# Four tiles in flight, transposes by DMA, and the threshold search moved to GpSimd

## Chip, cores, metric

One core of one Trainium2 chip. The metric is the device time of one launch in microseconds; of several runs the median is given.

## What is computed

2048 rows of 512 floats go through three blocks, each with a layer norm in front and a residual behind:

```python
x = x + 0.5 * lora_ffn(layernorm(x))   # FFN1: 64 experts of rank 16, top 16 by router score
x = x + glu(layernorm(x))              # gate, sparsify, up, down, width 1376
x = x + 0.5 * lora_ffn(layernorm(x))   # FFN3: the same weights as FFN1
# lora_ffn: scores = x @ Wr.T; gates = softmax(top 16 scores); h = x A.T;
#           out = (h * gates) B * 2
# glu: s = silu(x @ w_gate.T); in each row, the 688 smallest |s| of 1376 are set to 0;
#      out = (s * (x @ w_up.T)) @ w_down.T
```

## The kernel before

The rows are cut into 16 tiles of 128. All weights stay in SBUF, each as an f16 pair (hi, lo), and every product is three matmuls (`three`, lines 351 to 353: hi·hi, lo·hi, hi·lo). At the start each weight matrix is loaded in pieces, squared on ACT and summed on PE to find its scale, and split into hi (ACT, line 530) and lo (DVE, line 685). Then a loop of steps runs, i = 2 to 17. Step i does FFN1 and gate/up of tile i, finds the threshold of tile i-1, and does down and FFN3 of tile i-2. Every engine has its own in-order program; semaphores are the only order between engines.

PE, in a step: experts of FFN1 (`experts`, 24 matmuls of 512 columns and 12 of 64), `down` (33 matmuls), `combine` of FFN1 (24), experts of FFN3, the gate product and the up product (`wide`, 36 each), `combine` of FFN3. The three normed inputs are transposed on PE (`turn_x`, line 378, four f32 transposes each); the routed expert outputs and the masked values are transposed by DMA from SP's queue (`turn_p`, `turn_v`).

The threshold of a tile is found by seven counts on ACT (`count`, line 554: a Sign over 1376 columns with a sum) with six small correction steps between them (`search`, lines 755 to 759, four linked operations on 128x1 on DVE). `select` (lines 813 to 816) takes the exact threshold from the candidates, `mark` (lines 822 to 831) makes the mask, and branches to `bisect` if any row missed its count; for that it reduces flags and loads four values into registers. `mask` (863) multiplies, ACT casts to hi (584), DVE makes lo (876). The gate path is tanh on ACT (566), `silu` on DVE (847), `magnitude` on ACT (571), `gated` on DVE (855). GpSimd (POOL) does only the inverse square roots of the norms (`rstd`, lines 326 and 329).

`mag` has two buffers, so the magnitudes of tile i are made while the search on tile i-1 is in use. In DVE's program the six `search` steps stand between other work of the step:

```python
choose(1, i); median(0); route(1, i); median(1); apply_route(1, i); median(2)
p_split(1, i - 2); ...; norm_stats(3, x2); median(3); norm_apply(3, ...); median(4)
xt_to_lo(3, ...); ...; median(5); ...; select(i, b)
```

## Time and profile before

| | |
|---|---|
| median of 3 runs | 898.3 us (897.61 to 902.42) |
| the profiled execution | 900.5 us, its span 898.5 us |
| PE busy | 753.2 us, 84% |
| DVE busy | 571.4 us, 64% |
| ACT busy | 360.9 us, 40% |
| POOL busy | 36.3 us, 4% |
| mean granted TensorE clock | 0.943 of full speed |

The page's slices show three parts: a start of some 157 us, in which PE is busy for about half of the time; fourteen steps of about 46 us with PE at 90% and more; and two last steps, for tiles 14 and 15, in which PE is again half busy. A matmul's busy time overlaps with its neighbour's, so starts are compared, not durations.

### The profile page before, as it was taken

The page shows a single profiled execution, that of the slowest core. Times are in us where ns is not written, and L with a number is a line of the kernel's source. Part 1 is how long each engine was busy: PE and PEld are TensorE (multiplying, and loading weights), DVE is VectorE, ACT ScalarE, POOL GpSimd, SP SyncE. Part 2 cuts the span into 40 slices and gives each one's busy share as a digit, 9 for nine tenths or more (in the row PEclk, how much of TensorE's full clock was granted, in tenths as well). Part 3 has the DMA queues.
Part 4 walks back from the last instruction along what each step waited for, and adds up shares of the span by engine and source line. Part 5 has one row for each costly group of instructions (what it writes and reads, how often), then busy time and mean ns, then how long its engine had stood idle before and what let it go on. Part 6 is the DMA issues. An engine that isn't in the chain of part 4 may idle for free.

```text
span 898.5 us, 10482 instructions
## 1 busy us (share of the span) xinstructions
PE 753.2 (84%) x3863; PEld 356.3 (40%) x3863; DVE 571.4 (64%) x1403; ACT 360.9 (40%) x449; POOL 36.3 (4%) x104
## 2 busy tenths in 40 slices
PE   2766570999999898999999999999989999985555
PEld 0322230454545454444444444444444545442122
DVE  5355547576767676768686767676775767663521
ACT  4235574434343434343434343434434353433100
POOL 0000000000000000000000000000000000000000
PEclk9977795899999999999999999999999999997777
DMA  6332100213131313131312121212221221212121
GB/s 216 127 137 81 57 1 6 51 24 79 24 80 24 80 24 80 24 80 24 79 25 68 34 61 33 68 36 68 36 68 24 54 49 40 53 34 34 24 44 35
DMA packets 118922, 49.17 MB, mean 55 GB/s; under 512 B 110832, under 2 KB 110832, under 8 KB 118864
## 3 DMA queue, kind: packets, MB, share of 16 engines
q1 hardware_dynamic: 118864, 48.45, 22.8%
q8 instruction: 30, 0.49, 0.2%
q14 instruction: 28, 0.23, 0.1%
HBM read 16.97 MB, written 4.19 MB: 24 GB/s over the span
## 4 chain that ended last, share of the span: by engine, by line
PE 74%; DVE 10%; DMA 6%; issue 4%; ACT 4%; SPq 2%; DVEq 0%; POOL 0%; POOLq 0%; ACTq 0%
PE ps L351 24%; PE ps L352 23%; PE ps L353 23%; DMA vt_hi<-stage 3%; PE ps L378 2%; DVE xt_lo L702 1%; ACT xt_hi L535 1%; DMA pt_lo<-stage 1%; DMA stage<-w_a 1%; DMA vt_lo<-stage 1%; DVE y L931 1%; DVE w_d_lo L685 1%; PE ps L364 1%; ACT signs L554 1%; DVE small L655 1%
## 5 line engine op out<-in xcount | busy, mean ns | idle before, releaser
L554 ACT ACTIVATE signs<-mag,small 128x1376 bf16<-128x1376 f32 x112 | 161.4, 1441 | 144.8 <-DVE small L759 141.6
L351 PE MATMUL ps<-w_b_hi,pt_hi 128*128 128x512 f16 x256 | 100.0, 391 | 24.1 <-DMA pt_lo<-stage 16.5
L351 PE MATMUL ps<-w_d_hi,vt_hi 128*128 128x512 f16 x176 | 68.8, 391 | 38.3 <-issue 24.2
L351 PE MATMUL ps<-w_a_hi,xt_hi 128*128 128x512 f16 x256 | 100.3, 392 | 0.0
L352 PE MATMUL ps<-w_a_hi,xt_lo 128*128 128x512 f16 x256 | 100.0, 391 | 0.0
L352 PE MATMUL ps<-w_b_hi,pt_lo 128*128 128x512 f16 x256 | 99.9, 390 | 0.0
L353 PE MATMUL ps<-w_b_lo,pt_hi 128*128 128x512 f16 x256 | 99.7, 389 | 0.0
L353 PE MATMUL ps<-w_a_lo,xt_hi 128*128 128x512 f16 x256 | 99.6, 389 | 0.0
L351 PE MATMUL ps<-w_g_hi,xt_hi 128*128 128x512 f16 (+1 forms) x192 | 69.3, 361 | 8.7 <-DVE w_g_lo L685 6.1
L351 PE MATMUL ps<-w_u_hi,xt_hi 128*128 128x512 f16 (+1 forms) x192 | 69.4, 361 | 6.5 <-DVE w_u_lo L685 6.1
L352 PE MATMUL ps<-w_g_hi,xt_lo 128*128 128x512 f16 (+1 forms) x192 | 69.5, 362 | 0.0
L352 PE MATMUL ps<-w_u_hi,xt_lo 128*128 128x512 f16 (+1 forms) x192 | 69.5, 362 | 0.0
L353 PE MATMUL ps<-w_g_lo,xt_hi 128*128 128x512 f16 (+1 forms) x192 | 69.4, 361 | 0.0
L353 PE MATMUL ps<-w_u_lo,xt_hi 128*128 128x512 f16 (+1 forms) x192 | 69.3, 361 | 0.0
L352 PE MATMUL ps<-w_d_hi,vt_lo 128*128 128x512 f16 x176 | 69.0, 392 | 0.0
L353 PE MATMUL ps<-w_d_lo,vt_hi 128*128 128x512 f16 x176 | 68.7, 391 | 0.0
L890 DVE SCALAR_TENSOR_TENSOR x<-ps,small,x 128x512 f32<-128x512 f32 x16 | 12.0, 751 | 76.6 <-PE ps L353 76.6
L571 ACT ACTIVATE mag<-gate 128x1376 f32<-128x1376 f32 x16 | 21.6, 1350 | 86.2 <-DVE gate L847 86.2
L745 DVE TENSOR_TENSOR routed<-ps,weight 128x1024 f32<-128x1024 f32 x32 | 39.1, 1221 | 21.3 <-PE ps L353 21.3
L535 ACT ACTIVATE xt_hi<-ps 128x512 f16<-128x512 f32 x48 | 28.3, 590 | 56.4 <-PE ps L378 56.4
L566 ACT ACTIVATE gate<-ps,small 128x1376 f32<-128x1376 f32 x16 | 22.5, 1404 | 65.2 <-PE ps L353 65.2
L351 PEld LDWEIGHTS ps<-w_b_hi,pt_hi 128*128 128x128 f16 x256 | 25.6, 100 | 55.4 <-issue 31.2
(115 smaller groups left out, 1186.9 us busy)
## 6 DMA issues: line engine op xcount, KB each, us to landing
xin<-x SPq DMA_DIRECT2D x16, 256.0 KB, 3.0
out<-y SPq DMA_DIRECT2D x16, 256.0 KB, 2.0
stage<-w_g SPq DMA_DIRECT2D x4, 688.0 KB, 5.9
stage<-w_u SPq DMA_DIRECT2D x4, 688.0 KB, 5.9
stage<-w_d SPq DMA_DIRECT2D x5, 512.0 KB, 6.2
stage<-w_a SPq DMA_DIRECT2D x4, 512.0 KB, 7.2
stage<-w_b SPq DMA_DIRECT2D x4, 512.0 KB, 9.2
pt_hi<-stage SPq DMA_TRANSPOSE x30, 3.2
```

What stands on the lines that cost most here:

```text
L351: pe.matmul(dst, x_hi, w_hi, start=start, stop=False)
L352: pe.matmul(dst, x_lo, w_hi, start=False, stop=False)
L353: return pe.matmul(dst, x_hi, w_lo, start=False, stop=stop)
L364: mm = pe.matmul(bank(m.bank + o // BANK, w), ones[0:rows, :], sq[0:rows, q * m.width + o:q * m.width + o + w], start=c + q == 0, stop=c + ...
L378: mm = pe.transpose(bank(0, P, c * P), normed[j][:, c * P:(c + 1) * P], ident[:, :])
L535: act.activation(xt_hi[j][:, :, :], bank(0).rearrange("p (c t) -> p c t", c=DC), ACT.Copy).then_inc(xt_hi_ready[j], 1)
L554: act.activation(signs[:, :], mag[1 - b][:, :], ACT.Sign, bias=thr, scale=-1.0, accum_out=bal).then_inc(counted, 1)
L566: act.activation(gate[:, :], bank(2, I), ACT.Tanh, scale=unscale_g).then_inc(tanh_ready, 1)
L571: act.activation(mag[b][:, :], gate[:, :], ACT.Abs, accum_out=mag_sum).then_inc(mag_ready, 1)
L655: read = dve.tensor_reduce(norm2, bank(m.bank, m.width), AX.X, ALU.max)
L745: dve.tensor_tensor(routed[:, :].rearrange("p (k r) -> p k r", r=RANK), ps[:, 5 * BANK:5 * BANK + KR].rearrange("p (k r) -> p k r", r=RANK ...
L890: dve.scalar_tensor_tensor(out=x2[:, :], in0=bank(1), scalar=unscale_m, in1=x1[b][:, :], op0=ALU.mult, op1=ALU.add).then_inc(out_read, 1)
```

## The change

The loop is written anew. Step d (from -1 to 15) does down and FFN3 of tile d, the threshold, mask, up and `gated` of tile d+1, the gate product, `silu` and `magnitude` of tile d+2, the norm before the gate of tile d+3, FFN1 of tile d+5 and its norm for tile d+6 (`LEAD` = 4). FFN1 of tiles 0 to 4 stands in the start. From d = 11 on there is no FFN1 left, and `emit` takes its second branch on each engine.

- The inputs are split to f16 hi and lo in SBUF (`x_to_hi` ACT, `x_to_lo` DVE) and both halves are turned by one DMA transpose (`turn_x` on SP's queue), three more per tile. PE's transposes are gone.
- `search` and the first guess (`aim`) are on GpSimd, as six linked operations in place of four. All six searches of a tile stand one after another there, with `rstd(3, d)` after the third.
- There is one `mag`, one `val` and one `gate` buffer. Gate and up products share PSUM banks 2 to 4; the down product has bank 0, combine bank 1.
- `select` now works out whether the row failed; a matmul with ones adds the flags over the rows (`sum_flags`), and `check` loads one value and branches once. `mask` compares and multiplies in one operation.
- Weights b, g, u and d are loaded from GpSimd's queue, and GpSimd makes some of the lo pieces of g, u and d.
- x is loaded into nine slots, several tiles ahead, and results are added in place.

```diff
+LEAD = 4
+
+SLOTS = 9
...
+    calls = [(1, t) for t in range(LEAD + 1)]
+    for d in range(NT):
+        calls += [(1, d + LEAD + 1)] if d + LEAD + 1 < NT else []
+        calls += [(3, d)]
+    number = {c: k for k, c in enumerate(calls)}
...
+        DOWN, COMB, WIDE, EXP, SCORE = 0, 1, 2, 5, 7
...
+            def turn_x(j, t):
...
+                sp.dma_start_transpose(dst[:, :, :], halves[j]).then_inc(xt_loaded[j], 16)
...
+            def aim(t):
+
+                pool.wait_ge(mag_ready, t + 1)
+                link(pool.tensor_scalar(step, mag_sum, -SPACING / 2, None, ALU.mult))
+                pool.tensor_scalar(thr, mag_sum, GUESS, None, ALU.mult).then_inc(thr_ready, 1)
+
+            def search(t, n):
+
+                pool.wait_ge(counted, ROUNDS * t + n + 1)
+                link(pool.tensor_scalar(off, bal, -7.0, None, ALU.add))
+                link(pool.tensor_scalar(far, off, off, 7.5 ** 2, ALU.mult, ALU.is_gt))
+                link(pool.tensor_tensor(move, off, far, ALU.mult))
+                link(pool.tensor_tensor(move, move, step, ALU.mult))
+                link(pool.tensor_scalar(move, move, DAMP[n], None, ALU.mult))
+                pool.wait_ge(thr_ready, ROUNDS * t + n + 1)
+                pool.tensor_tensor(thr, thr, move, ALU.add).then_inc(thr_ready, 1)
+
+            def emit(d):
+                f = first(d)
+                for n in range(ROUNDS - 1):
+                    if n == 3 and d >= 0:
+                        rstd(3, d)
+                    if d + 1 < NT:
+                        search(d + 1, n)
+                if f is not None and f + 1 < NT:
+                    rstd(1, f + 1)
+                if d + 3 < NT:
+                    rstd(2, d + 3)
+                if d + 2 < NT:
+                    aim(d + 2)
+
...
+            def sum_flags(t):
+
+                if t:
+                    pe.wait_ge(x2_ready, t)
+                pe.wait_ge(flag_ready, t + 1)
+                pe.matmul(bank(DOWN, 1), ones[:, :], flag[:, 0:1], start=True, stop=True
+                          ).then_inc(flag_summed, 1)
+
+            def emit(d):
+                f = first(d)
+                if d >= 0:
+                    down(d)
+                if f is not None:
+                    experts(1, f)
+                if d == -1:
+                    norms(MD)
+                if d + 1 < NT:
+                    ups(d + 1, d == -1)
+                if f is not None:
+                    if d >= 0:
+                        experts(3, d)
+                    sum_flags(d + 1)
+                    combine(1, f)
+                    if d + 2 < NT:
+                        gates(d + 2)
                 else:
-                    turn_x(3, i - 2)
...
-            def search(i, n):
-
-
-                dve.wait_ge(counted, ROUNDS * (i - 1) + n + 1)
-                link(dve.tensor_scalar(off, bal, -7.0, None, ALU.add))
-                link(dve.tensor_scalar(far, off, off, 7.5 ** 2, ALU.mult, ALU.is_gt))
-                link(dve.scalar_tensor_tensor(out=move, in0=off, scalar=far, in1=step,
-                                              op0=ALU.mult, op1=ALU.mult))
-                dve.scalar_tensor_tensor(out=thr, in0=move, scalar=DAMP[n], in1=thr,
-                                         op0=ALU.mult, op1=ALU.add).then_inc(thr_ready, 1)
...
+            def select(t):
+
+
...
+                dve.wait_ge(counted, ROUNDS * (t + 1))
+                if t:
+                    dve.wait_ge(v_hi_ready, t)
+                    dve.wait_ge(v_lo_ready, t)
+                link(dve.scalar_tensor_tensor(out=masked[:, 0:I], in0=mag, scalar=thr, in1=mag,
+                                              op0=ALU.is_le, op1=ALU.mult))
+                link(dve.max(cand8, masked[:, 0:I]))
+                link(dve.scalar_tensor_tensor(out=top_a, in0=evens, scalar=bal, in1=cand8,
+                                              op0=ALU.is_equal, op1=ALU.mult, accum_out=kth))
+                link(dve.tensor_scalar(greater, cand8, kth, None, ALU.is_gt, ALU.add,
+                                       accum_out=above))
+                link(dve.scalar_tensor_tensor(out=wrong, in0=above, scalar=2.0, in1=bal,
+                                              op0=ALU.mult, op1=ALU.not_equal))
+                link(dve.scalar_tensor_tensor(out=wrong, in0=bal, scalar=15.0, in1=wrong,
+                                              op0=ALU.is_gt, op1=ALU.max))
+                if t:
+                    dve.wait_ge(flag_summed, t)
+                dve.scalar_tensor_tensor(out=flag[:, 0:1], in0=cand8[:, 0:1], scalar=thr,
+                                         in1=wrong, op0=ALU.is_equal, op1=ALU.max
+                                         ).then_inc(flag_ready, 1)
+
+            def mask(t):
+                dve.wait_ge(val_ready, t + 1)
+                link(dve.scalar_tensor_tensor(out=masked[:, 0:I], in0=mag, scalar=kth, in1=val,
+                                              op0=ALU.is_gt, op1=ALU.mult))
+
...
+            def check(t):
+                dve.wait_ge(flag_summed, t + 1)
+                link(dve.tensor_copy(flagged, bank(DOWN, 1)))
+                bad = dve.value_load(flagged[0:1, :], min_val=0, max_val=P)
+                with dve.If(bad != 0):
+                    bisect()
+                dve.memset(spare[:, 4:5], 0.0).then_inc(masked_ready, 1)
...
+            def emit(d):
+                f = first(d)
+                if f is not None:
+                    k1 = number[1, f]
+                    if d >= 0:
+                        k3 = number[3, d]
+                        if d >= 1:
+                            add_ffn(3, d - 1)
+                        add_down(d)
+                        norm_stats(3, d)
+                    choose(k1)
+                    if d >= 0:
+                        norm_apply(3, d)
+                    route(k1)
+                    if d >= 0:
+                        x_to_lo(3, d)
+                    apply_route(k1)
+                    p_to_lo(k1)
+                    select(d + 1)
+                    if d >= 0:
+                        choose(k3)
+                    gated(d + 1)
+                    if d >= 0:
+                        route(k3)
+                        apply_route(k3)
+                    mask(d + 1)
+                    if d >= 0:
+                        p_to_lo(k3)
+                    check(d + 1)
+                    v_to_lo(d + 1)
+                    add_ffn(1, f)
+                    if f + 1 < NT:
+                        norm_stats(1, f + 1)
+                    norm_stats(2, d + 3)
+                    if f + 1 < NT:
+                        norm_apply(1, f + 1)
+                        x_to_lo(1, f + 1)
+                    norm_apply(2, d + 3)
+                    x_to_lo(2, d + 3)
+                    silu(d + 2)
+                    return
+                k3 = number[3, d]
...
+                median(0, 1, 2, 3)
+                if f is not None:
+                    exps(number[1, f])
+                if d >= 0:
+                    x_to_hi(3, d)
+                if f is not None:
+                    median(4, 5)
+                    p_to_hi(number[1, f])
+                    median(6)
+                    if d >= 0:
+                        exps(number[3, d])
+                        p_to_hi(number[3, d])
+                    v_to_hi(d + 1)
+                    if f + 1 < NT:
+                        x_to_hi(1, f + 1)
+                    x_to_hi(2, d + 3)
+                    tanh(d + 2)
+                    magnitude(d + 2)
```

Where the instructions stand. First the search, on DVE before, within one step of the loop (L755 to L759 is one search step, L813 and L815 are `select`):

```order
L697 TENSOR_SCALAR normed<-x_0,mv,rvar 128x512
L736 SCALAR_TENSOR_TENSOR chosen,small<-work,expd 128x64
L739 RECIPROCAL small<-small 128x1
L740 TENSOR_SCALAR weight<-chosen,small 128x64
L755 TENSOR_SCALAR small<-small 128x1
L756 TENSOR_SCALAR small<-small 128x1
L757 SCALAR_TENSOR_TENSOR small<-small 128x1
L759 SCALAR_TENSOR_TENSOR small<-small 128x1
L702 TENSOR_TENSOR xt_lo<-ps,xt_hi 128x512
L745 TENSOR_TENSOR routed<-ps,weight 128x1024
L813 SCALAR_TENSOR_TENSOR stage<-mag,small 128x1376
L815 MAX small<-stage 128x8
```

And on GpSimd after the change (L395 to L401 is one search step, L379 and L383 are `rstd`):

```order
L399 TENSOR_SCALAR small<-small 128x1
L401 TENSOR_TENSOR small<-small 128x1
L379 TENSOR_SCALAR rvar<-mv 128x1
L383 TENSOR_TENSOR rvar<-rvar,neg_half 128x1
L395 TENSOR_SCALAR small<-small 128x1
L396 TENSOR_SCALAR small<-small 128x1
L397 TENSOR_TENSOR small<-small 128x1
L398 TENSOR_TENSOR small<-small 128x1
L399 TENSOR_SCALAR small<-small 128x1
L401 TENSOR_TENSOR small<-small 128x1
```

The search step went from four operations in DVE's program to six in GpSimd's, with nothing but `rstd` between one and the next. Second, DVE at the end of a step, before (L847 `silu`, L863 `mask`, L855 `gated`, L931 the residual of FFN3), from just behind the branch:

```order
L697 TENSOR_SCALAR normed<-xin,mv,rvar 128x512
L847 SCALAR_TENSOR_TENSOR gate<-gate,ps 128x1376
L863 TENSOR_TENSOR stage<-stage,keep 128x1376
L855 SCALAR_TENSOR_TENSOR stage<-gate,ps 128x1376
L859 TENSOR_SCALAR small<-small 128x1
L860 TENSOR_SCALAR small<-small 128x1
L702 TENSOR_TENSOR xt_lo<-ps,xt_hi 128x512
L931 SCALAR_TENSOR_TENSOR y<-ps,small,x 128x512
L876 TENSOR_TENSOR stage<-stage 128x1408
```

and after, also from just behind the branch (L968 `v_to_lo`, L857 residual of FFN1, L800 to L812 the norms and splits of the tiles to come, L870 `silu`):

```order
L962 MEMSET spare 128x1
L968 TENSOR_TENSOR mem<-mem 128x1408
L857 SCALAR_TENSOR_TENSOR x<-ps,small,x 128x512
L800 BN_STATS stats<-x 128x6
L801 BN_AGGR mv<-stats 128x2
L800 BN_STATS stats<-mem 128x6
L801 BN_AGGR mv<-stats 128x2
L805 TENSOR_SCALAR normed<-x,mv,rvar 128x512
L812 TENSOR_TENSOR halves<-normed,halves 128x512
L805 TENSOR_SCALAR normed<-mem,mv,rvar 128x512
L812 TENSOR_TENSOR halves<-normed,halves 128x512
L870 SCALAR_TENSOR_TENSOR mem<-mem,ps 128x1376
```

`silu` of the next tile, which the next search waits for, stood second behind the branch and is now the twelfth and last of the step.

## Rows read from the trace of the kernel before

**Rows 1.** Windows view: us of window, busy us of each engine, PE clock, DMA share, GB/s.

```profile
0.00:157.50 157.50, 83.08 (x369) 35.17 (x370) 83.85 (x184) 75.30 (x81) 4.56 (x18) 0.83 0.25 89
342.90:620.01 277.11, 264.87 (x1428) 129.24 (x1425) 197.18 (x492) 116.35 (x150) 13.28 (x36) 1.00 0.24 51
```

**Rows 2.** Timeline, ACT, one search round: start us, us, line, operation.

```profile
811.89 1.44 ACT L554 ACTIVATE signs<-mag,small 128x1376 bf16<-128x1376 f32 x1 [0.92 <-DVE small L759]
...
814.34 1.44 ACT L554 ACTIVATE signs<-mag,small 128x1376 bf16<-128x1376 f32 x1 [0.92 <-DVE small L759]
```

**Rows 3.** Timeline, DVE, the same round.

```profile
813.46 0.15 DVE L755 TENSOR_SCALAR small<-small 128x1 f32<-128x1 f32 x1 [1.60 <-ACT signs L554]
...
814.15 0.16 DVE L759 SCALAR_TENSOR_TENSOR small<-small 128x1 f32<-128x1 f32 x1
```

**Rows 4.** Timeline, POOL (GpSimd), one pair of small operations.

```profile
452.13 0.19 POOL L326 TENSOR_SCALAR rvar<-mv 128x1 f32<-128x1 f32 x1 [28.26 <-DVE mv L693]
452.40 0.55 POOL L329 TENSOR_TENSOR rvar<-rvar,neg_half 128x1 f32<-128x1 f32 x1
```

**Rows 5.** Groups by line, DVE: busy us, mean ns of one, idle before.

```profile
L745 DVE TENSOR_TENSOR routed<-ps,weight 128x1024 f32<-128x1024 f32 x32 | 39.1, 1221 | 21.3 <-PE ps L353 21.3
L702 DVE TENSOR_TENSOR xt_lo<-ps,xt_hi 128x512 f16<-128x512 f32 x48 | 32.9, 685 | 2.7 <-ACT xt_hi L535 2.1
L813 DVE SCALAR_TENSOR_TENSOR stage<-mag,small 128x1376 f32<-128x1376 f32 x16 | 26.3, 1642 | 2.2 <-ACT signs L554 2.2
L863 DVE TENSOR_TENSOR stage<-stage,keep 128x1376 f32<-128x1376 f32 x16 | 25.4, 1585 | 6.8 <-issue 6.8
L692 DVE BATCH_NORM_STATS2 stats<-x 128x6 f32<-128x512 f32 x32 | 22.2, 694 | 1.1
L697 DVE TENSOR_SCALAR normed<-x,mv,rvar 128x512 f32<-128x512 f32 x32 | 17.5, 546 | 5.3 <-POOL rvar L329 4.8
L890 DVE SCALAR_TENSOR_TENSOR x<-ps,small,x 128x512 f32<-128x512 f32 x16 | 12.0, 751 | 76.6 <-PE ps L353 76.6
```

**Rows 6.** Groups by line, ACT.

```profile
L549 ACT ACTIVATE stage<-routed 128x1024 f16<-128x1024 f32 x30 | 31.5, 1050 | 23.2 <-DVE routed L745 23.2
L566 ACT ACTIVATE gate<-ps,small 128x1376 f32<-128x1376 f32 x16 | 22.5, 1404 | 65.2 <-PE ps L353 65.2
L571 ACT ACTIVATE mag<-gate 128x1376 f32<-128x1376 f32 x16 | 21.6, 1350 | 86.2 <-DVE gate L847 86.2
```

**Rows 7.** Timeline, DVE, around the branch of line 831.

```profile
424.97 0.18 DVE L828 TENSOR_REDUCE ints<-flags_t 128x1 int32<-128x32 f32 x1
428.81 0.55 DVE L697 TENSOR_SCALAR normed<-xin,mv,rvar 128x512 f32<-128x512 f32 x1 [3.66 <-issue]
```

**Rows 8.** Timeline, DVE, choose and route of tile 14, last tile but one.

```profile
829.45 0.23 DVE L723 COPY scores<-ps 128x64 f32<-128x64 f32 x1 [0.98 <-PE ps L353]
...
831.75 0.15 DVE L755 TENSOR_SCALAR small<-small 128x1 f32<-128x1 f32 x1
```

**Rows 9.** Timeline, PE, matmuls after a pause.

```profile
858.67 0.58 PE L351 MATMUL ps<-w_d_hi,vt_hi 128*128 128x512 f16 x1 [6.75 <-DMA vt_lo<-stage]
859.05 0.63 PE L352 MATMUL ps<-w_d_hi,vt_lo 128*128 128x512 f16 x1
859.47 0.63 PE L353 MATMUL ps<-w_d_lo,vt_hi 128*128 128x512 f16 x1
```

**Rows 10.** Timeline, PE, matmuls later in the same stretch.

```profile
866.80 0.38 PE L351 MATMUL ps<-w_d_hi,vt_hi 128*128 128x512 f16 x1
867.02 0.38 PE L352 MATMUL ps<-w_d_hi,vt_lo 128*128 128x512 f16 x1
```

**Rows 11.** Chain that ended last: select of tile 0 and of tile 15.

```profile
143.00 1.66 DVE stage L813
...
836.87 1.57 DVE stage L813
```

**Rows 12.** DMA view: transposes, KB and median us to landing.

```profile
pt_lo<-stage SPq DMA_TRANSPOSE x30, 3.1
vt_lo<-stage SPq DMA_TRANSPOSE x16, 3.9
```

1209 lines of the change are left out of this document (590 added, 619 removed).

## The prediction, made before the change was run

> **What bounds the kernel now.** I read the windows first. In the six steps from 342.90 to 620.01 us a step takes 277.11 / 6 = 46.2 us, with 264.87 / 6 = 44.1 us of PE busy at full clock [rows 1]: PE bounds the steps. In the first 157.5 us it is busy for only 83 us [rows 1], since there it waits for weights to be scaled and split. The chain of waits gives the frame for the sum. `select` of tile 0 starts at 143.0 and that of tile 15 at 836.9 [rows 11]: 15 intervals of 46.3 us, and behind the last one 898.5 - 836.9 = 61.6 us. So the span is start + 15 intervals + tail = 143.0 + 693.9 + 61.6.
>
> The timelines show what a search costs alone. One Sign count starts 2.45 us behind the other [rows 2]; DVE's four operations take 0.85 of that, from 813.46 to 814.31 [rows 3]. In the steps this is hidden: there are two `mag` buffers, and DVE's other work stands between the six search steps.
>
> **PE's work after the change.** The transposes of x leave. Matmuls of 512 columns follow each other at 0.215 us at full clock [rows 10]. A step has 177 of them, 24 of 352 columns (0.15, by columns) and 24 of 64 (0.03): 38.1 + 3.6 + 0.7 = 42.4 us. If PE still bounded the steps, 3.8 us of 46.2 would go. The question is whether anything else takes over.
>
> **The new cycle.** With one `mag` buffer, `magnitude` of tile t+1 must follow `mask` of tile t, and the search on t+1 must follow that; DVE's program puts twelve pieces of work between `select` and `silu`. I follow one interval of a full step from the start of `select` on, in us, all in series on DVE unless named:
> - `select`: two passes over 1376 (1.64 and about the same [rows 5]) and five small operations (0.2 to 0.3 each, as in [rows 3]): 4.6.
> - choose and route of FFN3: 831.75 - 829.45 = 2.3 [rows 8]. `gated` 1.5, `apply_route` 1.15, `mask` 1.6 [rows 5]; `p_to_lo` of 1024 elements 1.15, as `apply_route`. Together 7.7.
> - `check`: a copy and a memset 0.4, and one load with its branch. Now four loads and the branch leave DVE idle for 3.66 us [rows 7]. One costs between a quarter of it (0.9) and all of it; I take 1.5, nearer the quarter since three of four loads are gone. 1.9.
> - `v_to_hi` on ACT 1.45 (like the tanh of nearly the same size, [rows 6]), then `v_to_lo` 1.55: 3.0.
> - `add_ffn` 0.75, two stats with their aggregates 1.75, and 0.1 of waiting for POOL [rows 4, 5]: 2.6.
> - Norm and hi/lo of two inputs in turn, ACT between: 0.5 + 0.65 + 0.65 + 0.5 + 0.65 [rows 5]; hi of 512 elements is priced from 1.05 for 1024 [rows 6]: 3.0.
> - tanh 1.45 [rows 6], `silu` 1.65, `magnitude` 1.6 with its accumulator read [rows 6], `aim` on POOL 0.6 (two operations 0.27 apart [rows 4], and a crossing): 5.3.
>
> That is 28.1. Then the search, which nothing shortens: seven counts and six steps. A count with its read is 813.43 - 811.89 = 1.54 [rows 2, 3]. On POOL a linked tensor_scalar costs 0.27 from start to start [rows 4]. No row shows a plain tensor_tensor there. It is bounded by the tensor_scalar's 0.19 and by the 0.55 of the power function [rows 4]; I take 0.25, nearer the lower end, because the power is another function, while DVE's small operations hardly differ with their operands [rows 3]. A step: 3 x 0.27 + 2 x 0.33 + 0.25 = 1.72 (1.54 to 2.62). With 0.15 for the two crossings a round is 1.54 + 1.72 + 0.15 = 3.41 (3.23 to 4.31), against 2.45 now. The search: 6 x 3.41 + 1.6 = 22.1. **A full interval is 50.2 us**, 4 longer than now.
>
> The page "GPSIMD Engine Reference" of the Trainium skill (section 3.1, Elementwise) measures a two-input tensor_tensor at 1.96 times DVE's time; an estimate by it puts one at 0.16 x 1.96 = 0.31, the interval at 51.3 and the time at 921. No row here shows it.
>
> PE is covered by this. From `sum_flags` (4.8 behind `select`) it does combine 5.2 and the gate product 7.0, so tanh could start at 17.2, but ACT comes to it only at 22.7. `down`, both experts and the up product also fit; PE would idle for some 7.8 us a step. The DMA transposes need 3.1 to 3.9 us each [rows 12], are issued four and more us ahead of their use except for the input of FFN3, whose experts PE reaches about 4 us too early, and that wait ends before the flags are ready. SP's queue holds nine issues in 50 us. The other work DVE does ahead of `select` (norms, routing of FFN1) lies beside the counts.
>
> **Last steps and ends.** From d = 11 on FFN1 is gone and `silu` stands right behind `v_to_lo`: 4.6 + 1.6 + 2.2 + 3.0 + 1.6 + 1.6 + 0.6 + 22.1 = 37.3. The intervals are: the first without FFN3's part, 50.2 - 4.6; ten full ones; the last with FFN1 without the norm of a next tile, 50.2 - 2.9; three of 37.3. Sum 45.6 + 502.0 + 47.3 + 111.9 = 706.8, where 693.9 stood.
>
> Start: three more tiles of FFN1 (16 us at full clock before the first `magnitude`) go into PE's idle time, and loads run ahead; against this, ACT squares and splits w_d before it counts, POOL makes three lo pieces (no row for such an operation there), and the seven counts no longer overlap. I keep 143, with 10 to either side, and 20 shorter as a rival.
>
> Tail: `select` to the down product is 15.5 (4.6 + 1.6 + 2.2 + 3.0 and 4.1 for the DMA) where 858.67 - 836.87 = 21.8 stood [rows 9, 11]; turning the input of FFN3 by DMA costs 2.4 more. 61.6 - 6.3 + 2.4 = 57.7.
>
> Span 143 + 706.8 + 57.7 = 907.5. The profiled execution takes 2.0 more than its span (900.5 against 898.5) and lies 2.2 above the median, so the median comes to 907.5 + 2.0 - 2.2 = 907.3: **908 us**. Each us of the full interval is worth 12. The point of balance is 49.4.
>
> **Rivals.**
> 1. GpSimd's small operations are cheaper when linked one to another than the pair shown: at 0.2 each from start to start a step is 1.2, a round 2.9, the interval 47.1, the time **871**. It decides from a round of 3.28 down, close to the low end of my bound. For it: DVE's own chain has gaps of 0.04 only. Against: 0.27 is measured on the same kind of link [rows 4].
> 2. GpSimd and DVE collide. `x_to_lo` of FFN3 (0.69) and `p_to_lo` (1.22) [rows 5] fall into a search step, and each may hold it for its length: up to 1.9 an interval, **931**. Nothing in the trace speaks for or against; POOL is busy for 36 us in all and never beside such an operation. The Trainium skill, page "SBUF — State Buffer", section "SBUF: two separate sides", says that a DVE operation with two SBUF inputs and a GpSimd operation lock each other out for a whole instruction, which is this case.
> 3. PE falls to half clock in its new gaps. After a pause of 6.75 us matmuls follow at 0.42 to 0.43 instead of 0.215 [rows 9, 10]. Two pauses of 3 to 4 us a step are short, and 5.5 us of slack hide a few slow matmuls; if combine and gate product ran wholly at half clock (24.4 instead of 12.2), the interval would grow by 6.7: **988**, or 948 if in every second step.
> 4. The start shrinks by 20: the products for five tiles fill it and the counts begin right behind `magnitude`: **888**. PE's 74 idle us [rows 1] speak for it, ACT's order against.
> 5. Tensor_tensor on GpSimd has the price of the power function, 0.55: round 4.31, interval 55.6, **973**.
> 6. The order of DVE does not bind, and PE bounds: 42.4 to 43 a full interval, about **820**. The serial walk speaks against it.
>
> **How the numbers follow.** This kernel's measurement can tell about 0.5% (4.5 us) from no change. Chances: forecast 0.40 (its own range 896 to 920; 0.12 of it within 0.5%, the rest slower), rival 1 0.20, rival 2 0.17, rival 3 0.07, rival 4 0.08, rival 5 0.04, rival 6 0.04. Faster 0.32, same 0.12, slower 0.56. The range, 868 to 962, leaves out rival 6, what of rival 1 goes beyond its price, and rivals 5 and 3 at their worst, some 0.2 in all.
>
> **What would show it.** Right: `select` to `select` 50 us in the middle; POOL busy for over 130 us; ACT's counts 3.4 us apart without a break, waiting for POOL; PE at 84% in the steps, with waits at the flag matmul and at the experts of FFN3; 37 us intervals at the end. Wrong: counts under 3.2 or over 3.7 apart; tanh waiting for PE instead of ACT's own order; PE over 95% busy; a first `select` before 130 or after 155.

## The result, and the profile after

| | before | after |
|---|---|---|
| median | 897.95 us (896.99 to 902.42) | 948.19 us (945.28 to 949.11) |
| ratio | | 1.054, 95% interval 1.050 to 1.059 |
| span of the profiled execution | 898.5 us | 947.3 us |
| PE / DVE / ACT / POOL busy | 84 / 64 / 40 / 4% | 79 / 51 / 38 / 25% |
| mean granted TensorE clock | 0.943 | 0.908 |

The change makes the kernel 5.4% slower; I had forecast 908 us, 1.1% slower. The windows answer [rows 1]: us of the window, busy us of PE, PEld, DVE, ACT and POOL, the TensorE clock, DMA share, GB/s. The first window is the start up to the first `select`, the second ten full steps.

```profile
0.00:162.67 162.67, 86.95 (x403) 35.96 (x403) 86.92 (x183) 75.09 (x81) 68.66 (x90) 0.84 0.44 117
210.32:717.85 507.53, 449.67 (x2260) 208.56 (x2260) 274.32 (x580) 194.12 (x250) 120.21 (x440) 0.94 0.31 61
```

POOL is busy for 68.66 us in the start, where it had been busy for 4.56. A full step is now 50.75 us. The chain that ended last gives the frame, as in [rows 11]: start us, duration, `select` (L889) of tiles 0, 1, 2, 7, 8, 11 to 15.

```profile
162.67 1.66 DVE mem L889
210.32 1.66 DVE mem L889
260.77 1.66 DVE mem L889
...
514.55 1.67 DVE mem L889
565.25 1.66 DVE mem L889
...
717.85 1.67 DVE mem L889
765.43 1.66 DVE mem L889
808.85 1.66 DVE mem L889
852.30 1.66 DVE mem L889
891.52 1.67 DVE mem L889
```

Set against the sum of the prediction:

| part | forecast | measured | difference |
|---|---|---|---|
| start, to the first `select` | 143.0 | 162.7 | +19.7 |
| first interval | 45.6 | 47.6 | +2.0 |
| ten full intervals | 502.0 | 507.5 | +5.5 |
| last interval with FFN1 | 47.3 | 47.6 | +0.3 |
| three late intervals | 111.9 | 126.1 | +14.2 |
| tail | 57.7 | 55.8 | -1.9 |
| span | 907.5 | 947.3 | +39.8 |

So the long middle is as forecast, and 34 of the missing 40 us lie in the start and in the late intervals. The first interval is 2.0 over its forecast too; what it lost was not traced. The timelines show the rest.

**The search round** (ACT, then POOL; answers to [rows 2] and [rows 4]; start us, us):

```profile
545.41 1.44 ACT L645 ACTIVATE signs<-mem,small 128x1376 bf16<-128x1376 f32 x1 [1.84 <-POOL small L401]
...
548.78 1.44 ACT L645 ACTIVATE signs<-mem,small 128x1376 bf16<-128x1376 f32 x1 [1.84 <-POOL small L401]
```

```profile
543.65 0.21 POOL L395 TENSOR_SCALAR small<-small 128x1 f32<-128x1 f32 x1 [1.65 <-ACT signs L645]
543.96 0.30 POOL L396 TENSOR_SCALAR small<-small 128x1 f32<-128x1 f32 x1
544.34 0.19 POOL L397 TENSOR_TENSOR small<-small 128x1 f32<-128x1 f32 x1
544.61 0.19 POOL L398 TENSOR_TENSOR small<-small 128x1 f32<-128x1 f32 x1
544.88 0.22 POOL L399 TENSOR_SCALAR small<-small 128x1 f32<-128x1 f32 x1
545.18 0.19 POOL L401 TENSOR_TENSOR small<-small 128x1 f32<-128x1 f32 x1
```

A round is 3.37 us (forecast 3.41), the six operations 545.18 + 0.19 - 543.65 = 1.72 (forecast 1.72). That the second number comes out to the hundredth is luck. I had the three tensor_scalars too cheap: from start to start they take 0.31, 0.38 and 0.30, not 0.27 each, since `L396`, with a column as scalar, takes 0.30 by itself. And I had the three tensor_tensors too dear: they take 0.19 like a plain tensor_scalar, not 0.25. The two errors are 0.18 each and cancel.

**The collision.** At the end of the same search POOL (first fence) and DVE (second):

```profile
561.88 1.21 POOL L398 TENSOR_TENSOR small<-small 128x1 f32<-128x1 f32 x1
```

```profile
561.81 1.22 DVE L850 TENSOR_TENSOR p_lo<-routed,p_hi 128x1024 f16<-128x1024 f32 x1 [5.14 <-ACT p_hi L640]
```

An operation of 0.19 us stands for 1.21, until `p_to_lo` ends. Rival 2 was built on the Trainium skill, page "SBUF — State Buffer", section "SBUF: two separate sides": a DVE operation with two inputs in SBUF, or one in a 2-port mode, and a GpSimd operation that reads SBUF shut each other out for the whole instruction. The trace agrees for the first kind. One search pays 1.0 for this and 0.3 for `x_to_lo` of FFN3. From first count to `select` it takes 23.2 us (542.03 to 565.25) where 22.1 were forecast.

**The branch** (DVE, answers to [rows 7]): one load and branch leave 1.54 us idle, for which I had 1.5.

```profile
526.68 0.15 DVE L958 CAST ints<-ps 128x1 int32<-128x1 f32 x1
528.37 0.06 DVE L962 MEMSET spare<- 128x1 f32 x1 [1.54 <-issue]
```

**The start.** POOL makes seven lo pieces, two operations each. Here are the two operations of the first piece of w_g, the rstd that stands behind both pieces of w_g, and the first operation of a piece of w_u; then DVE:

```profile
67.23 3.81 POOL L372 TENSOR_SCALAR mem<-mem,small 128x1376 f32<-128x1376 f32 x1 [15.52 <-ACT w_g_hi L622]
71.12 2.79 POOL L373 TENSOR_TENSOR w_g_lo<-mem,w_g_hi 128x1376 f16<-128x1376 f32 x1
...
80.61 0.19 POOL L379 TENSOR_SCALAR rvar<-mv 128x1 f32<-128x1 f32 x1
...
98.55 3.76 POOL L372 TENSOR_SCALAR mem<-mem,small 128x1376 f32<-128x1376 f32 x1
```

```profile
81.56 0.55 DVE L805 TENSOR_SCALAR normed<-x,mv,rvar 128x512 f32<-128x512 f32 x1 [16.86 <-POOL rvar L383]
...
98.58 4.01 DVE L805 TENSOR_SCALAR normed<-x,mv,rvar 128x512 f32<-128x512 f32 x1 [0.97 <-POOL rvar L383]
...
103.17 7.98 DVE L783 SCALAR_TENSOR_TENSOR w_u_lo<-mem,small,w_u_hi 128x1376 f16<-128x1376 f32 x2
```

Such a piece costs POOL 6.6 us (3.81 + 2.79), against 1.6 on DVE (3.21 for the two that it makes at 83.15). DVE waits 16.86 us for an rstd that was queued behind two pieces. Later DVE's own operations stretch beside POOL's: 4.01 instead of 0.55, 7.98 instead of 3.2. The first search then waits for the pieces of w_d: count 0 is at 130.74, its step at 141.26, count 1 at 143.16.

**The late intervals** (ACT, step of tile 12's `select` at 765.43):

```profile
777.52 1.35 ACT L657 ACTIVATE mem<-mem 128x1376 f32<-128x1376 f32 x1 [1.90 <-DVE mem L870]
...
781.42 1.06 ACT L640 ACTIVATE p_hi<-routed 128x1024 f16<-128x1024 f32 x1 [2.12 <-DVE routed L840]
786.10 0.63 ACT L629 ACTIVATE halves<-normed 128x512 f16<-128x512 f32 x1 [3.63 <-DVE normed L805]
786.64 1.43 ACT L645 ACTIVATE signs<-mem,small 128x1376 bf16<-128x1376 f32 x1
```

`magnitude` ends at 779, but ACT's program has exps and `p_to_hi` of FFN3 and `x_to_hi(2)` ahead of the next count, and each waits for DVE. The first count comes 21.2 us after `select`; the walk of the prediction had 15.2.

### The profile page after: what moved, and what is told of

It reads as the page before. It is cut to its first block, busy times and chain, and to the rows that moved or that the text cites. A ratio compares the mean times of both kernels' runs of the same rounds, so it can differ in the third digit from the quotient of the medians.

```text
span 947.3 us, 10462 instructions
## 1 busy us (share of the span) xinstructions
PE 752.4 (79%) x3671; PEld 341.7 (36%) x3671; DVE 487.4 (51%) x1008; ACT 361.3 (38%) x447; POOL 241.4 (25%) x742
## 4 chain that ended last, share of the span: by engine, by line
DVE 30%; ACT 24%; POOL 20%; issue 14%; PE 7%; DMA 3%; DVEq 1%; POOLq 0%; SPq 0%; ACTq 0%
ACT signs L645 14%; POOL small L398 3%; POOL small L396 3%; DVE mem L889 3%; DVE small L891 3%; DVE mem L870 3%; DVE mem L968 3%; POOL small L399 2%; DVE routed L840 2%; PE ps L454 2%; POOL small L395 2%; ACT mem L663 2%; POOL small L397 2%; PE ps L455 2%; ACT mem L657 2%
## 5 line engine op out<-in xcount | busy, mean ns | idle before, releaser
L645 ACT ACTIVATE signs<-mem,small 128x1376 bf16<-128x1376 f32 x112 | 161.4, 1441 | 189.3 <-POOL small L401 181.6
L454 PE MATMUL ps<-w_a_hi,xt_f 128*128 128x512 f16 x256 | 102.4, 400 | 8.4 <-DVE routed L840 6.0
L455 PE MATMUL ps<-w_a_hi,xt_f 128*128 128x512 f16 x256 | 101.8, 398 | 0.0
L456 PE MATMUL ps<-w_a_lo,xt_f 128*128 128x512 f16 x256 | 100.9, 394 | 0.0
L379 POOL TENSOR_SCALAR rvar<-mv 128x1 f32<-128x1 f32 x48 | 9.1, 190 | 338.7 <-DVE mv L801 336.3
L454 PE MATMUL ps<-w_d_hi,mem 128*128 128x512 f16 x176 | 68.8, 391 | 9.9 <-DMA mem<-mem 9.9
L850 DVE TENSOR_TENSOR p_lo<-routed,p_hi 128x1024 f16<-128x1024 f32 x32 | 39.2, 1224 | 69.1 <-ACT p_hi L640 68.7
L454 PE MATMUL ps<-w_g_hi,xt 128*128 128x512 f16 (+1 forms) x192 | 68.5, 357 | 0.9 <-DVE mem L876 0.8
L455 PE MATMUL ps<-w_d_hi,mem 128*128 128x512 f16 x176 | 68.9, 391 | 0.0
L454 PE MATMUL ps<-w_u_hi,xt 128*128 128x512 f16 (+1 forms) x192 | 68.5, 357 | 0.0
L456 PE MATMUL ps<-w_g_lo,xt 128*128 128x512 f16 (+1 forms) x192 | 68.5, 357 | 0.0
L456 PE MATMUL ps<-w_u_lo,xt 128*128 128x512 f16 (+1 forms) x192 | 68.5, 357 | 0.0
L455 PE MATMUL ps<-w_u_hi,xt 128*128 128x512 f16 (+1 forms) x192 | 68.5, 357 | 0.0
L455 PE MATMUL ps<-w_g_hi,xt 128*128 128x512 f16 (+1 forms) x192 | 68.5, 357 | 0.0
L456 PE MATMUL ps<-w_d_lo,mem 128*128 128x512 f16 x176 | 68.4, 388 | 0.0
L395 POOL TENSOR_SCALAR small<-small 128x1 f32<-128x1 f32 x96 | 20.7, 215 | 147.0 <-ACT signs L645 146.9
```

What stands on the lines that cost most here:

```text
L395: link(pool.tensor_scalar(off, bal, -7.0, None, ALU.add))
L454: pe.matmul(dst, x_hi, w_hi, start=start, stop=False)
L455: pe.matmul(dst, x_lo, w_hi, start=False, stop=False)
L456: return pe.matmul(dst, x_hi, w_lo, start=False, stop=stop)
L645: act.activation(signs[:, :], mag, ACT.Sign, bias=thr, scale=-1.0, accum_out=bal).then_inc(counted, 1)
L850: dve.tensor_tensor(p_lo[:, :], routed[:, :], p_hi[:, :], ALU.subtract).then_inc(p_lo_ready, 1)
```

## Experiments

Each ratio is to the kernel before, with its 95% interval; all but e6 start from the changed kernel. "Full interval" is from `select` to `select` in the middle steps, "late" the three last (43.42, 43.45 and 39.22 in the changed kernel).

**e1: all lo pieces on DVE.**

```diff
-    MG = Matrix("g", DC, I, 1, P, AT_G, 2, (1, 3))
+    MG = Matrix("g", DC, I, 1, P, AT_G, 2, ())
-    MU = Matrix("u", DC, I, 1, P, 0, 2, (1, 3))
+    MU = Matrix("u", DC, I, 1, P, 0, 2, ())
-    MD = Matrix("d", IC, D, 2, LAST, AT_G, 0, (1, 3, 5))
+    MD = Matrix("d", IC, D, 2, LAST, AT_G, 0, ())
...
-            split_lo(MG, 1)
-            split_lo(MG, 3)
...
-            split_lo(MU, 1)
-            split_lo(MU, 3)
```

> The changed kernel, with all lo pieces of the weights made on DVE again (seven pieces less on GpSimd). Theory (GpSimd's pieces lengthen the start: 13.2 us of pieces of w_g stand ahead of rstd, and DVE waits 16.9 us for it; pieces of w_d stand ahead of the first search step, and ACT waits 10.9 us): the first select starts at 143 to 148 instead of 162.7, the intervals behind it stay, and the time is 928 to 934. Rival (the start is bound by the loads and by PE's work for five tiles, the waits only show where the slack is): first select at 158 or later, 943 to 948.

Measured: 922.9 us, ratio 1.029 (1.022 to 1.036). The first `select` starts at 134.58 instead of 162.67, and nothing else moves (full intervals 50.7, late 43.4, 43.4, 39.2). The gain is larger than expected, but not all of the 28.1 us of the start is due to the pieces. The third rstd, which stands ahead of the first piece, starts at 31.39 in the changed kernel's profiled execution and at 27.90 in this one. From it to the first `select` there are 131.3 and 106.7 us. So the pieces cost 24.6 us, which fits the medians (948.2 - 922.9 = 25.3). That is all of the excess of the start over my 143, and 5 more.

**e2: the search step in four GpSimd operations.**

```diff
-                link(pool.tensor_tensor(move, off, far, ALU.mult))
-                link(pool.tensor_tensor(move, move, step, ALU.mult))
-                link(pool.tensor_scalar(move, move, DAMP[n], None, ALU.mult))
+                link(pool.tensor_scalar(move, far, off, step, ALU.mult, ALU.mult))
                 pool.wait_ge(thr_ready, ROUNDS * t + n + 1)
-                pool.tensor_tensor(thr, thr, move, ALU.add).then_inc(thr_ready, 1)
+                pool.tensor_scalar(thr, move, DAMP[n], thr, ALU.mult, ALU.add).then_inc(thr_ready, 1)
```

> The changed kernel, with a search step of four GpSimd operations instead of six, for the same result: the product of three factors and the damped sum are one tensor_scalar each with two scalars. Theory (the six rounds are in series with everything else in every interval): the rounds go from 3.38 to about 2.9 us, each interval loses 6 x 0.5 = 3 us, 16 searches give 48 us, and the time is 900 (895 to 908). Rival A (PE bounds the steps and the waits for the flags only show slack): within 5 us of 948. Rival B (GpSimd's two-scalar operations cost more than they save): 940 to 955.

Measured: 914.5 us, ratio 1.019 (1.016 to 1.022), of the expected gain 34 us instead of 48. POOL's timeline shows one step:

```profile
528.69 0.22 POOL L395 TENSOR_SCALAR small<-small 128x1 f32<-128x1 f32 x1 [1.66 <-ACT signs L643]
529.01 0.29 POOL L396 TENSOR_SCALAR small<-small 128x1 f32<-128x1 f32 x1
529.40 0.34 POOL L397 TENSOR_SCALAR small<-small 128x1 f32<-128x1 f32 x1
529.84 0.26 POOL L399 TENSOR_SCALAR small<-small 128x1 f32<-128x1 f32 x1
```

A step is 1.41 us: the operation with two columns as scalars costs 0.34 and the one with a column and a constant 0.26, more than the plain ones that they replace. A round is 3.07 and the full interval 48.8, so each 0.31 us of a round is worth 1.9 to 2.0 an interval: the search is in series with everything, as the prediction has it.

**e4: `p_to_lo` with one input in memory** (the low half of p is replaced by a scaled copy of `routed`, so that this part is not computed).

```diff
-                dve.tensor_tensor(p_lo[:, :], routed[:, :], p_hi[:, :], ALU.subtract
+                dve.tensor_scalar(p_lo[:, :], routed[:, :], unscale_r, 0.0, ALU.mult, ALU.mult
```

> The changed kernel, with p_lo made from routed alone by a tensor_scalar (one SBUF input instead of two; the low halves of the routed values are not what the reference needs, so the precision of both FFN blocks changes). Theory (a DVE operation with two SBUF inputs shuts GpSimd out): the one long GpSimd operation in every search (L398, 1.21 us where its neighbours take 0.19) falls back to about 0.2, intervals with FFN1 lose 1.0 us, 12 us in all: 936. Rival (the long operation has another cause, such as its place behind five rounds): L398 keeps one of 1.2 us in every search and the time stays at 948.

Measured: 935.5 us, ratio 1.042 (1.038 to 1.046); the full interval is 49.94. The time fits by luck: the trace shows another reason than the expected one. `p_to_lo` takes 0.75 us instead of 1.22, and POOL's operation beside it still stands for all of it:

```profile
504.93 0.73 POOL L398 TENSOR_TENSOR small<-small 128x1 f32<-128x1 f32 x1
```

So the form with one input holds POOL too, for as long as it runs. Whether this is the 2-port mode that the Trainium skill names, no run here tells. The 0.8 us that an interval wins are about what `p_to_lo` is shorter by, 0.47 in DVE's chain and 0.48 in POOL's.

**e5: the late order of ACT.**

```diff
-                median(0, 1, 2, 3)
+                if d >= 1 and first(d - 1) is None:
+                    median(0)
+                    exps(number[3, d - 1])
+                    median(1)
+                    p_to_hi(number[3, d - 1])
+                    median(2, 3)
+                    if d + 2 < NT:
+                        x_to_hi(2, d + 2)
+                else:
+                    median(0, 1, 2, 3)
```

On POOL rstd(2) of these steps stands behind search 2, ahead of search 3.

> Edit: in the late steps only (those without an FFN1 of a later tile), exps and the high half of the routing of the tile's FFN3, and x_to_hi(2), are taken out of ACT's program ahead of the next search and stand behind its counts 0, 1 and 3; rstd(2) goes with search 3 on GpSimd. Theory: the three late intervals are 43.42, 43.45 and 39.22 us because count 0 of the next search stands behind exps, p_to_hi and x_to_hi(2), which wait for TensorE, though aim was done 6 to 7 us sooner (aim about 780, first count 786.64); freed of that they take 37 to 38 us each, as forecast: 933 us (930 to 937). Rival: TensorE's FFN3 of the tile waits for the high half of p that comes later now and the end moves by as much: 945 to 950.

Measured: 944.1 us, ratio 1.050 (1.046 to 1.054); the late intervals are 41.43, 41.43 and 37.52, together 5.7 us less. (The span of the profiled execution is only 1.9 less, 945.4. Its first `select` is at 167.70, and its third rstd is already 4.8 later than in the changed kernel, with the same instructions up to there.) The first half of the theory holds: the first count comes 14.2 us behind `select` instead of 21.2. But 5 of these 7 us are lost again inside the search. TensorE's waits did not grow (flag 5.09 and 4.55 us in the first two late steps, where it was 5.08 and 5.08, and 1.1 and 1.3 for the transposed values where it was 2.7 and 2.3), so it is not the rival either. DVE's timeline, then POOL's:

```profile
797.05 0.55 DVE L815 TENSOR_SCALAR normed<-x,mv,rvar 128x512 f32<-128x512 f32 x1 [4.14 <-POOL rvar L383]
```

```profile
796.17 0.19 POOL L379 TENSOR_SCALAR rvar<-mv 128x1 f32<-128x1 f32 x1
...
800.68 0.19 POOL L379 TENSOR_SCALAR rvar<-mv 128x1 f32<-128x1 f32 x1 [3.66 <-DVE mv L811]
```

I had put rstd(2) a search step too late on POOL. DVE stood for it, reached the addition and the norm of FFN3 late, and rstd(3) of that norm stands ahead of the next search step: count 4 followed count 3 by 7.75 us. e9 has this mended.

**e7: the search back on DVE**, in the four operations of the kernel before, at six places of DVE's program.

```diff
+                    search(d + 1, 0, 1)
                     if d >= 0:
                         add_down(d)
                         norm_stats(3, d)
                     choose(k1)
+                    search(d + 1, 2)
                     if d >= 0:
                         norm_apply(3, d)
+                    search(d + 1, 3)
                     route(k1)
                     if d >= 0:
                         x_to_lo(3, d)
                     apply_route(k1)
+                    search(d + 1, 4)
                     p_to_lo(k1)
+                    search(d + 1, 5)
```

> Edit: the change with only its search step put back on DVE in the four instructions of the kernel before, at hand-chosen places of DVE's program (two steps ahead of add_down, one behind choose, one behind norm_apply, one behind apply_route, one behind p_to_lo); the overlap of four tiles, the lead and the DMA turns stay. Theory: a round takes 3.38 us on GpSimd and took 2.45 on DVE, so six rounds give 5.6 us of the 50.7 back wherever the search sets the interval, less what DVE's other work holds a step up; TensorE at about 45 to 48 then bounds the full intervals: 48 x 11, three late ones 5 less each, first one 5 less, start 2 less: 948 - 30 - 15 - 7 = 896 us (885 to 908), so the move of the search alone is all of the loss and the overlap of four tiles is worth nothing beside the kernel before. Rival: the long interval comes from the order of the tail (routing, check, norms, silu in a row), which stays: the steps on DVE are held up by its other work and no more than 20 us come back, 928 to 948.

Measured: 894.5 us, ratio 0.994 (0.991 to 0.997). The number is as expected: with the search on DVE the whole loss is gone, and the kernel is 0.6% below the one before. But the move of the search is not the only loss. In the profiled executions this kernel's start is still 17.1 us longer than before (160.05 against 143.00), its 15 intervals are 10.4 shorter and its tail is 6.1 shorter, and e1 won 25 us with the search left on GpSimd. So the change had two large losses, search and start, and gains in the loop and the tail that cover about one of them. What the DMA transposes, the longer lead and the single buffers are worth one by one was not tried. The full interval is 47.9 and the late ones are 38.64, 38.03 and 39.35. Not each round is short, since DVE's other work holds steps up (ACT's counts):

```profile
521.93 1.44 ACT L632 ACTIVATE signs<-mem,small 128x1376 bf16<-128x1376 f32 x1 [0.92 <-DVE small L961]
...
524.38 1.44 ACT L632 ACTIVATE signs<-mem,small 128x1376 bf16<-128x1376 f32 x1 [0.92 <-DVE small L961]
...
528.26 1.44 ACT L632 ACTIVATE signs<-mem,small 128x1376 bf16<-128x1376 f32 x1 [2.35 <-DVE small L961]
```

**e6: the kernel before with only its search on GpSimd**, in the six operations of the change, with the two `mag` buffers and the old order kept (POOL's program; DVE's calls of `search` go).

```diff
+                median(0, 1, 2)
                 rstd(3, i - 2, turn)
+                median(3, 4)
                 if cur:
                     rstd(2, i, turn + 1)
+                median(5)
```

> The kernel before, with its six search steps moved to GpSimd as in the change, and nothing else. Theory (a search step on GpSimd costs 0.9 us more, but in the kernel before the search lies beside other work, with two buffers for mag): within 5 us of 898, the rounds that stand alone at the end give the few us, PE stays at 44 of 46 us. Rival (GpSimd's steps cost by themselves, wherever they stand: 6 x 0.9 us an interval): 960 to 980.

Measured: 934.9 us, ratio 1.043 (1.038 to 1.047). Both numbers miss. I had thought that two buffers hide a longer search, since the search of one tile is not in series with the making of the next. Steps are 47.8 us for 46.1, with some of 50 to 53. The waits of TensorE (us in total, times, longest), first before, then e6:

```profile
PE ps L351 <- DVE xt_lo L702: 33.2, 19, 16.6
```

```profile
PE ps L379 <- DVE xt_lo L730: 64.2, 19, 19.1
```

TensorE waits 31 us longer for lo halves of inputs, about the 33 us by which the span grew. ACT makes hi halves between its counts: at 459.06 it counts, the next count waits for POOL until 467.16, whose step stood behind an rstd at 464.15, and the hi half of FFN3's input follows at 468.60. A late search step thus reaches TensorE through ACT's queue. How much of this is the price of the steps, and how much the two places of rstd between them, was not tried.

**e3 and e11: the next gate early.** In full steps `silu` of the next tile moves on DVE right behind `v_to_lo`, tanh and `magnitude` on ACT go ahead of `x_to_hi(1)` and `x_to_hi(2)`, `aim` on POOL ahead of the rstds. e3 on ACT, and then e11 against e3 on DVE:

```diff
+                if d >= 0 and first(d - 1) is not None:
+                    median(0)
+                    if first(d - 1) + 1 < NT:
+                        x_to_hi(1, first(d - 1) + 1)
+                    median(1)
+                    x_to_hi(2, d + 2)
+                    median(2, 3)
...
-                    if f + 1 < NT:
-                        x_to_hi(1, f + 1)
-                    x_to_hi(2, d + 3)
                     tanh(d + 2)
                     magnitude(d + 2)
```

```diff
                     v_to_lo(d + 1)
-                    silu(d + 2)
                     add_ffn(1, f)
+                    silu(d + 2)
```

> Edit: in the full steps only, the next tile's gate is made ready sooner. On DVE silu(d+2) stands right behind v_to_lo(d+1) instead of behind add_ffn, the two normed and the two halves of x; on ACT tanh and magnitude stand ahead of x_to_hi(1) and x_to_hi(2), which move behind count 0 and count 1 of the next search; on GpSimd aim stands ahead of the two rstd. The work and its cost stay the same. Theory: the full interval of 50.7 us is a chain through DVE (select, choose, route, V, add_ffn, norms, silu) into ACT and GpSimd, so 5 us of work taken out of the chain shorten each of the 11 full intervals by about 5: 893 us (885 to 905). Rival 1: TensorE's work and the granted clock (busy 449.67 of 507.5 us over ten intervals, clock 0.94) bound the interval at about 45 to 46 already, and the moved high halves come late for TensorE, which then waits for them instead: at most 1 us each, 937 to 948. Rival 2: the search shares its engine ACT with the moved halves, and the rounds grow by what they take: no gain, 945 to 955.

> Edit: e3 (tanh, magnitude and silu of the next tile early, search in six operations, low halves still shared with GpSimd) with add_ffn of FFN1 ahead of silu on DVE instead of behind it, and nothing else. Theory: what e3 lacked to its forecast was TensorE's wait of 3.9 us in each full step for the bank that this add frees, with the fall of the granted clock that goes with waits; without it the full interval is the search's again, 44.66 of the combined kernel plus six rounds times 0.31: 46.5 us instead of 49.5, 11 of them: 934 - 33 = 901 us (893 to 912). Rival: the combined kernel needed the shorter rounds for its gain, and with 3.38 us in a round the order of the add matters by its own 0.7 us at most: 925 to 940.

Measured: e3 934.2 us, ratio 1.040 (1.037 to 1.043); e11 926.4 us, ratio 1.032 (1.029 to 1.034). Full intervals are 49.6 (in turn 48.9 and 50.0) and 48.5 where 45.7 and 46.5 were expected. In e3 two things go wrong in a row, on PE and then on POOL:

```profile
530.67 0.58 PE L456 MATMUL ps<-w_b_hi,pt_hi 128*128 128x512 f16 x1 [3.87 <-DVE x L864]
```

```profile
546.52 0.19 POOL L379 TENSOR_SCALAR rvar<-mv 128x1 f32<-128x1 f32 x1 [3.29 <-DVE mv L808]
```

TensorE waits for the bank that `add_ffn` frees, `down` comes late, and the search stands behind rstd(3), which waits for it. e11 takes this away, and its interval still doesn't reach 46.5. What is left is a loop through TensorE, read under e9.

**e8: everything together**: e1, e2, e3 and e5 in one kernel.

> Edit: the early silu, the late order, the search step of four operations and the low halves of the weights on DVE, all in one kernel. Theory: the gains add as long as DVE, ACT and GpSimd's chain is the bound: start 132 to 135, first interval 43, eleven full intervals near 44 where the chain alone asks for 50.7 - 1.9 - 5 = 43.8 and TensorE was busy for 45.0 in each at clock 0.94, so 45 to 46 each, late ones 35.5 each, tail 55: 134 + 43 + 11 x 45.5 + 106.5 + 55 = 839 us (825 to 860), faster than the kernel before (898). Rival: the gains do not add, since TensorE waits for the same flags in another place or its clock falls when it stands in longer stretches of waiting: 870 to 900, no better than the kernel before.

Measured: 877.8 us, ratio 0.978 (0.974 to 0.981). Faster than before, but 39 over the expectation: full intervals of 48.2 instead of 45.5 (the wait of e3, 3.9 us a step) and late ones of 39.6, 39.6 and 35.5 (the misplaced rstd(2) of e5).

**e9: e8 with both mended.** On DVE the pair of e11; on POOL and ACT, in the late steps, against e8:

```diff
-                    if n == 3 and d >= 1 and first(d - 1) is None and d + 2 < NT:
+                    if n == 2 and d >= 1 and first(d - 1) is None and d + 2 < NT:
                         rstd(2, d + 2)
...
-                    median(2, 3)
+                    median(2)
                     if d + 2 < NT:
                         x_to_hi(2, d + 2)
+                    median(3)
```

> Edit, on the combined kernel (877.8 us): on DVE add_ffn of FFN1 stands ahead of silu(d+2) instead of behind it; in the late steps rstd(2) stands ahead of search 2 on GpSimd instead of behind it, and x_to_hi(2) behind count 2 instead of count 3. Theory: TensorE waits 3.9 us in each full step for the bank that this add_ffn frees, while DVE waits for tanh ahead of it; with the add first the wait falls to about 1.5, and as TensorE bounds the full step there (44.35 of 48.22 us busy) 2.3 us are won in each of 11; in the late steps DVE stood 4.1 us behind rstd(2), of which 3 to 3.5 come back in three of them: 877.8 - 25 - 10 = 843 us (837 to 855). Rival: the chain through gate, tanh, silu and the search is the bound and not TensorE, so that moving the add (0.74 us) ahead of silu only delays the chain: full intervals 48.2 to 49, 868 to 886.

Measured: **841.0 us, ratio 0.935 (0.929 to 0.941)**, as expected, the fastest kernel of the study. All full intervals are 44.65 to 44.70, the late ones 37.23, 37.23 and 35.45. TensorE is close to being the bound (the window 230 to 650, columns as above):

```profile
230.00:650.00 420.00, 400.90 (x2101) 189.46 (x2102) 259.02 (x545) 180.46 (x232) 104.50 (x291) 1.00 0.36 68
```

That is 95% busy at full clock, and [rows 1] had the same 95% at 46.2 us a step: here the transposes are gone from TensorE. But it is not the bound by itself. It is busy for 42.9 of the 44.66 us of a step and still waits 1.05 for the flags, and tanh waits 1.8 for it: the interval is a loop through search, flags, gate product and tanh.

Beside e11 this shows the loop. For each of three kernels, the changed one, e11 and e9, follow TensorE's wait at the flag matmul (timeline) and then the window of the 12.4 us behind it (combine and gate product):

```profile
519.16 0.16 PE L556 MATMUL ps<-flag,ones 128*128 128x1 bf16 x1 [5.47 <-DVE flag L902]
```

```profile
519.15:531.55 12.40, 12.39 (x49) 5.22 (x50) 9.11 (x19) 2.87 (x3) 0.00 (x0) 0.82 0.26 52
```

```profile
505.94 0.16 PE L558 MATMUL ps<-flag,ones 128*128 128x1 bf16 x1 [3.85 <-DVE flag L909]
```

```profile
505.93:518.33 12.40, 12.39 (x51) 5.36 (x52) 9.11 (x19) 2.87 (x3) 0.00 (x0) 0.86 0.26 51
```

```profile
498.12 0.16 PE L554 MATMUL ps<-flag,ones 128*128 128x1 bf16 x1 [1.05 <-DVE flag L913]
```

```profile
498.12:510.52 12.40, 12.40 (x61) 5.87 (x61) 9.11 (x19) 2.87 (x3) 0.00 (x0) 1.00 0.27 52
```

Behind a wait of 3.85 or 5.47 us the granted clock of the stretch is 0.86 or 0.82, a mixture of the levels 2.4 and 1.2 GHz; behind 1.05 it is 1.00, and 61 matmuls fit in where 49 to 51 did. In the changed kernel tanh starts 22.4 behind `select` with no idle time of ACT before it, so it waits for ACT's own order. In e11 and e9 ACT stands idle before tanh, for 3.2 to 5.0 us in e11 and mostly 1.8 in e9, until the gate product ends: now that product is in the loop. In e11 tanh starts 18.8 us behind `select` (501.33 to 520.10) and the next `select` 29.5 later; in e9 it is 17.1 (493.52 to 510.61) and 27.6. The second difference is the search, 6 x 0.31 as expected; the first is the clock. So 0.31 us of a round cost 1.9 us directly and 1.7 through the wait and the clock behind it.

**e10: e9 with the search on DVE**, placed as in e7, but with its first steps in the tail of the step before, as the early gate asks for:

```diff
                     norm_apply(2, d + 3)
+                    search(d + 2, 0)
                     x_to_lo(2, d + 3)
...
                 apply_route(k3)
+                search(d + 2, 0)
                 p_to_lo(k3)
```

> Edit: the kernel of e9 with the search on DVE in four instructions instead of on GpSimd, spread over DVE's program as in e7. Theory: full intervals are TensorE's and stay as in e9; the first interval, the late ones and the start are the search's, with rounds of 2.45 us instead of 3.07: about 3.7 less in four intervals and 3 less at the start: 18 us below e9, about 825 us (815 to 840). Rival: DVE's work between the counts (choose 1.9 us, apply_route 1.2, add_down with its wait for TensorE) holds the search up by more than the 3.7 us: at or above e9.

Measured: 874.5 us, ratio 0.972 (0.966 to 0.978): the rival was right, and by far. Full intervals are 47.8, the late ones 40.4, 40.1 and 36.7. From the first count to `select` the search takes 24.0 us (535.78 to 559.82) against 22.5 in e9 (515.74 to 538.20): only one of six rounds has 2.46, the others 3.2 to 4.5, since a step stands behind choose, `apply_route`, `p_to_lo` or an addition on DVE. The flag wait is 3.49 us, and tanh starts 18.6 behind `select` (17.1 in e9), as in e11. The 1.5 us of the search and the 1.5 up to tanh are the whole difference of the intervals. So with the early gate GpSimd is a better place for the search than these places in DVE's program, though its operations are slower. Other places on DVE were not tried.

## Why the prediction was right or wrong, point by point

- **The frame and the direction** were right: start, 15 intervals, tail, with the search in series. e2 shows it: 0.31 us of a round move the interval by 1.9. That it is the single `mag` buffer that puts the search in series was argued and not tried.
- **The full interval**, 50.2: measured 50.7. The round, the branch and the order on ACT ahead of tanh came out, the search step (1.72) by errors that cancel. The collision, rival 2, I had as an alternative with a chance of 0.17: it happens, and adds 1.3 to an interval, not 1.9. It belonged into the forecast, with 16 us in 12 intervals. The interval is off by 0.5 only because the path from `select` to the first count is 27.5 (514.55 to 542.03) where I had 28.1, and the rounds are a little shorter than 3.41.
- **The start**: "I keep 143, with 10 to either side". This step failed, by 19.7 us. I counted "three lo pieces" on POOL, of w_d, and left out two of w_g and two of w_u, gave them no price and did not walk what is queued behind them. e1 puts the cost at some 25 us; without them the start would be about 138 (162.7 - 24.6), so the 143 itself was fair.
- **The late intervals**: "4.6 + 1.6 + 2.2 + 3.0 + 1.6 + 1.6 + 0.6 + 22.1 = 37.3". This step failed, by 14.2 us in three intervals. I followed DVE's order alone, where `silu` stands right behind `v_to_lo`. ACT's order has three operations ahead of the count. In the full steps I had walked ACT's order as well, and there the walk was right. The whole excess lies there: from `select` to the first count the three intervals have 21.2, 21.2 and 16.9 us, while their searches take 22.2 to 22.3, as forecast. e9, with that order mended, has 14.2 to the first count and an interval of 37.2. That it meets my 37.3 is in part luck: its round is 0.31 shorter, while the work of FFN3 that now stands between the counts holds the search up again (23.1 us in all).
- **PE at half clock**, rival 3: partly true. The stretch behind the flag wait had a mean clock of 0.82, not half. In the changed kernel it cost little, since tanh waited for ACT anyway; in e11 it cost 1.7 us an interval.
- **"The point of balance is 49.4"**: wrong, as the start and the late steps were mis-sized. With these as measured the balance lies at 50.7 - 50 / 12 = 46.5.
- **The other rivals**: GpSimd's chained operations are 0.27 to 0.38 from start to start, not the 0.2 of rival 1, and a tensor_tensor is far from the 0.55 of rival 5. The start grew instead of shrinking (rival 4); only without POOL's pieces is it some 5 us shorter. TensorE as the bound (rival 6) is what e9 comes close to, at 44.7 us instead of 42.4 to 43.
- **The signs that I named**: the first `select` is behind 155, which I had as a sign of being wrong. TensorE is busy for 89% of the full steps (449.67 of 507.53), not 84%, as it runs at a clock of 0.94 and stands idle for 5.8 us a step instead of 7.8. It waits at the flag matmul for 5.47, and not at the experts of FFN3. ACT's counts are 3.38 apart and wait for POOL, as forecast.

The two misses are of one kind: the full interval, walked through on all engines, was right to some 1%, the parts that were taken over from the kernel before or walked on one engine were 13 to 14% off.

## What to carry to other kernels

- Walk start and end of a pipelined kernel like its middle, on every engine: for each waiting instruction ask what its own engine has ahead of it, not only who releases it. Here most of 34 us lay in queues that the middle doesn't have.
- Work on an idle engine is not free when it stands ahead of small results others wait for: with seven pieces on GpSimd the start was some 25 us longer than with the same pieces on DVE.
- A slow chain and a throttled TensorE feed each other: from e11 to e9 TensorE's wait falls from 4 to 1 us, and the gain is twice what the chain alone gives. The same search on GpSimd was worth -6% in one order and better than the one tried order on DVE in another (841 against 874), so an engine should be judged after the order, not before it.
